# A quarter of the additions of states into y in a selective-scan kernel go from VectorE to ScalarE and GpSimd

## The reference

```python
u, gate = split(xn @ W_in.T)                       # D = 1024 channels each
u = silu(causal_conv4(u) + conv_b)
dt, B, C = (rmsnorm(p) for p in split(u @ Wx.T))    # 32, N = 16, N = 16
delta = softplus(dt @ Wdt.T + dt_bias)
state = exp(delta * A) * state + delta * u * B      # for each of D x N states, along 512 tokens
y = sum over n of C[n] * state[n]  +  u * D_param
s = (y * silu(gate)) @ W_out.T
g = silu((silu(xn @ w_gate.T) * (xn @ w_up.T)) @ w_down.T)
x = x + s * g
```

## Time and profile before

| | us |
|---|---|
| median of 3 runs | 1310.66 (1310.46 to 1311.51) |
| the profiled execution | 1310.51 |
| its span, first to last instruction | 1308.6 |
| VectorE busy | 1160.3 (89%) |
| TensorE busy | 1109.4 (85%) |
| GpSimd busy | 950.5 (73%) |
| ScalarE busy | 665.7 (51%) |

### The profile page before, as it was taken

One profiled execution on the slowest core, in us unless ns is written; L12 is line 12 of the kernel. 1 busy time (PEld: TensorE's weight loads), 2 busy tenths in 40 slices (PEclk: granted clock), 3 DMA queues, 4 the chain that ended last, 5 costly groups with the idle time before them and its releaser, 6 DMA issues.

```text
span 1308.6 us, 16506 instructions
## 1 busy us (share of the span) xinstructions
PE 1109.4 (85%) x5072; PEld 777.8 (59%) x5072; DVE 1160.3 (89%) x1436; ACT 665.7 (51%) x1000; POOL 950.5 (73%) x440
## 2 busy tenths in 40 slices
PE   5859985789959987988987997998995998986977
PEld 4647764655647765564656765665564776544544
DVE  5359999998979999999798999999797999999893
ACT  4557543654476643465375843465447664443330
POOL 3488985777678996577579897576767899755731
PEclk9879996699969998999997999899996999996979
DMA  4112231212302231322222232232221222221411
GB/s 131 66 49 88 88 117 38 66 56 73 105 28 95 89 129 49 129 81 91 79 76 79 76 121 81 93 109 73 73 105 28 94 90 97 90 96 57 129 48 65
DMA packets 42789, 108.78 MB, mean 83 GB/s; under 512 B 4843, under 2 KB 5099, under 8 KB 42700
## 3 DMA queue, kind: packets, MB, share of 16 engines
q1 hardware_dynamic: 42700, 107.69, 24.8%
HBM read 103.35 MB, written 4.33 MB: 82 GB/s over the span
## 4 chain that ended last, share of the span: by engine, by line
PE 31%; DVE 24%; POOL 22%; issue 17%; ACT 3%; DMA 1%; DVEq 1%; POOLq 0%
POOL sb_dBu L578 13%; DVE sb_h L816 11%; PE pj L861 8%; PE pj L1069 7%; DVE sb_yT L742 6%; PE hT L1109 6%; PE pj L1093 3%; POOL sb_v L550 3%; POOL sb_delta L544 3%; DVE sb_un L661 3%; POOL sb_w_lo L533 2%; PE pj L1123 2%; PE pj L1036 2%; PE pj L866 2%; PE pj L878 1%
## 5 line engine op out<-in xcount | busy, mean ns | idle before, releaser
L578 POOL TENSOR_TENSOR sb_dBu<-sb_v,sb_bb 128x1024 f32<-128x1024 f32 x256 | 607.4, 2388 | 166.2 <-DVE sb_h L816 161.5
L816 DVE TENSOR_TENSOR_SCAN sb_h<-dA,sb_dBu 128x512 f32<-128x512 f32 x512 | 595.7, 1204 | 46.6 <-POOL sb_dBu L578 28.9
L439 ACT ACTIVATE dA<-sb_delta,sb_apar 128x512 f32<-128x512 f32 x512 | 352.4, 691 | 543.4 <-DVE sb_h L816 538.1
L1109 PE MATMUL hT<-sb_ident,sb_h 128*128 128x128 f32 x2048 | 310.0, 294 | 145.2 <-DVE sb_yT L742 128.0
L1109 PEld LDWEIGHTS hT<-sb_ident,sb_h 128*128 128x128 f32 x2048 | 251.8, 150 | 247.4 <-DVE sb_yT L742 137.9
L742 DVE SCALAR_TENSOR_TENSOR sb_yT<-hT,sb_cs,sb_yT 128x512 f32<-128x512 f32 x476 | 330.1, 734 | 35.7 <-PE hT L1109 35.0
L533 POOL TENSOR_TENSOR sb_w_lo<-sb_ring,sb_w_hi 128x1024 fp32r<-128x1024 f32 x76 | 181.6, 2390 | 79.9 <-ACT sb_w_hi L331 79.5
L861 PE MATMUL pj<-sb_x_hi,sb_w_lo 128*128 128x512 f32 x608 | 188.6, 434 | 26.6 <-DVE sb_un L661 16.3
L861 PE MATMUL pj<-sb_x_lo,sb_w_hi 128*128 128x512 f32 x608 | 172.3, 407 | 0.0
L861 PE MATMUL pj<-sb_x_hi,sb_w_hi 128*128 128x512 f32 x608 | 165.9, 395 | 0.0
L861 PEld LDWEIGHTS pj<-sb_x_hi,sb_w_lo 128*128 128x128 f32 x608 | 108.5, 198 | 74.6 <-issue 22.6
(11 more groups left out here) (100 smaller groups left out, 819.0 us busy)
## 6 DMA issues: line engine op xcount, KB each, us to landing
sb_ring<-w_ring SPq DMA_DIRECT2D x116, 512.0 KB, 3.3
sb_bb<-b_rows SPq DMA_DIRECT2D x128, 256.0 KB, 3.2
sb_xio<-x SPq DMA_DIRECT2D x8, 1024.0 KB, 6.4
out<-sb_xio SPq DMA_DIRECT2D x3, 1024.0 KB, 5.6
out<-sb_xio SPq DMA_DIRECT2D x4, 256.0 KB, 2.0
sb_wx<-w_x SPq DMA_DIRECT2D x1, 256.0 KB
sb_wdt<-w_dt SPq DMA_DIRECT2D x1, 132.0 KB
b_rows<-sb_dtB SPq DMA_DIRECT2D x4, 32.0 KB, 1.6
```

Source lines behind the costliest of these rows:

```text
L439: nc.scalar.activation(dA[g % 2][:, :], delta[:, j, :], ACT.Exp, scale=apar[:, j, n:n + 1]).then_inc(dA_done, 1)
L578: nc.gpsimd.tensor_tensor(dBu[:, dbu_buffer(s), :, :], v[:, j:j + 2, :], bb[:, i % B_RING, :].unsqueeze(1).to_broadcast([P, 2, T]), ALU.mu ...
L816: nc.vector.tensor_tensor_scan(h[:, i % 2, 2 * part + e, :], dA[g % 2][:, :], dBu[:, dbu_buffer(s), e, :], 0.0, ALU.mult, ALU.add).then_in ...
L1109: done = nc.tensor.transpose(hT[c % H_BANKS][:, j * P:(j + 1) * P], h[:, i % 2, j, c * P:(c + 1) * P], ident[:, :])
```

## The change

Block c = 3 of each unit is handed over (`handed_over` returns (3,) for every unit). VectorE adds blocks 0, 1 and 2 as before. For block 3 ScalarE multiplies the transposed block by C (Copy with a scale by partition, from a copy cs_act of C of its own) in its slot 2i + 3, after `side` and ahead of `round_entry`: for n = 0 straight into yT, else into one of two buffers `part`. GpSimd adds the buffer to yT in its slot 2i + 5, after dBu and w_lo and ahead of the gate products. Of unit 31 of the last batch nothing is handed over. TensorE waits for ScalarE's semaphore `ev_done` where the bank was freed by a product, and for GpSimd's `yp_done` as well before it transposes y back. In batches 1 to 3 the products of unit 31 fall into slot 1, and the sums of units 30 and 31 into slots 1 and 3. To make room in SBUF, the conv buffer cth is laid over the first two tiles of v.

```diff
+def handed_over(u):
+    return (3,)
+OFF = [(u, c) for u in range(UNITS) for c in handed_over(u)]
+OFF_ADDS = [(u, c) for u, c in OFF if u % N > 0]
+ON = [(u, c) for u in range(UNITS) for c in range(TC) if (u, c) not in OFF]
...
-        cth = sb("cth", [P, 2, T])
+        part = sb("part", [P, 2, H])
+        cs_act = sb("cs_act", [P, TC, N])
...
+        cth = v[:, 0:2]
...
+                def take_state(c_b, i, c, no_first):
+                    hf, n = i // N, i % N
+                    act.wait_ge(hT_ps, c_b * UNITS * TC + i * TC + c + 1)
+                    if n == 0:
+                        if not no_first:
+                            act.wait_ge(yb_ps, (c_b - 1) * KD + (hf + 1) * JH)
+                        dst = yT[:, c, hf * JH * P:(hf + 1) * JH * P]
+                    else:
+                        q = OFF_ADDS.index((i, c))
+                        if not (no_first and q < 2):
+                            act.wait_ge(yp_done, c_b * len(OFF_ADDS) + q - 1)
+                        dst = part[:, q % 2, :]
+                    nc.scalar.activation(dst, hT[c % H_BANKS][:, :], ACT.Copy, scale=cs_act[:, c, n:n + 1]).then_inc(ev_done, 1)
...
                 for s in range(SLOTS):
                     decay(s)
                     side(s)
+                    for i, c in OFF:
+                        if s == 2 * i + 3:
+                            take_state(b, i, c, first)
+                        elif s == 2 * i + 3 - SLOTS and not first:
+                            take_state(b - 1, i, c, False)
+                    if s == 2 and not first:
+                        act.wait_ge(nrm_done, (b + 1) * 2)
+                        act.wait_ge(ev_done, b * len(OFF))
+                        nc.scalar.copy(cs_act[:, :, :], nrm[:, :, G + N:FN]).then_inc(csa_done, 1)
+                        act.wait_ge(csa_done, b + 1)
                     if s in HI_AT and not (last and HI_AT[s][1] >= U0):
                         round_entry(b, *HI_AT[s])
...
+            def add_part(c_b, i, c):
+                q, hf = OFF_ADDS.index((i, c)), i // N
+                pool.wait_ge(ev_done, c_b * len(OFF) + done_by(OFF, i, c))
+                before = [p for p in range(q) if OFF_ADDS[p][1] == c and OFF_ADDS[p][0] // N == hf]
+                if before:
+                    pool.wait_ge(yp_done, c_b * len(OFF_ADDS) + before[-1] + 1)
+                y = yT[:, c, hf * JH * P:(hf + 1) * JH * P]
+                nc.gpsimd.tensor_tensor(y, y, part[:, q % 2, :], ALU.add).then_inc(yp_done, 1)
...
+                    for m, c in OFF_ADDS:
+                        if s == 2 * m + 5:
+                            add_part(b, m, c)
+                        elif s == 2 * m + 5 - SLOTS and not first:
+                            add_part(b - 1, m, c)
...
-                        if i > 0:
+                        if i > 0 and (i - 1, c) in ON:
                             add_state(b, i - 1, c)
-                        elif not first:
+                        elif i == 0 and not first and (UNITS - 1, c) in ON:
                             add_state(b - 1, UNITS - 1, c)
...
                         if j == JH:
-                            pe.wait_ge(y_done, b * UNITS * TC)
+                            pe.wait_ge(y_done, b * len(ON))
+                            pe.wait_ge(yp_done, b * len(OFF_ADDS))
                             pe.wait_ge(za_done, b * KD + JH)
```

More of the change, by code:

```diff
@@ L49, with done_by @@
 ORDINAL = {k: o for o, k, s in SPLITS}
+def handed_over(u):
[3 more added lines that the diff above has]
+ON = [(u, c) for u in range(UNITS) for c in range(TC) if (u, c) not in OFF]
+def done_by(acts, u, c):
+    return len([a for a in acts if a <= (u, c)])
 def dbu_buffer(s):
@@ L614, in _ @@
             sequences(pool, sequence)
+            for m, c in OFF_ADDS:
+                if SLOTS <= 2 * m + 5 and m < UNITS - 1:
+                    add_part(NB - 1, m, c)
             for j in range(JH, KD):
@@ L829, in _ @@
                 dve.wait_ge(hT_ps, b * UNITS * TC + i * TC + c + 1)
-                dve.wait_ge(y_done, b * UNITS * TC + (i - 1) * TC + c + 1)
+                if (i - 1, c) in ON:
+                    dve.wait_ge(y_done, b * len(ON) + done_by(ON, i - 1, c))
+                else:
+                    dve.wait_ge(yp_done, (b + 1) * len(OFF_ADDS) - len(handed_over(i)) - len(handed_over(i - 1)) + done_by([(i - 1, d) for d in handed_over(i - 1)], i - 1, c))
                 y = yT[:, c, JH * P:D]
@@ L1105, in sequence @@
                     for c in (2 * part, 2 * part + 1):
-                        if not (first and i == 0 and c < 2):
-                            pe.wait_ge(y_done, b * UNITS * TC + i * TC + c - 1)
+                        before = (i, c - H_BANKS) if c >= H_BANKS else (i - 1, c + TC - H_BANKS)
+                        if not first or before[0] >= 0:
+                            if before in ON or (UNITS - 1, before[1]) in ON and before[0] < 0:
+                                pe.wait_ge(y_done, b * len(ON) + (done_by(ON, *before) if before[0] >= 0 else done_by(ON, UNITS - 1, before[1]) - len(ON)))
+                            else:
+                                pe.wait_ge(ev_done, b * len(OFF) + (done_by(OFF, *before) if before[0] >= 0 else done_by(OFF, UNITS - 1, before[1]) - len(OFF)))
                         for j in range(JH):
```

15 lines of the change are left out of this document (11 added, 4 removed).

## The result

The changed kernel takes 1339.0 us (median of 4 runs, 1337.2 to 1339.9), the kernel before 1311.1 beside it (4 runs, 1310.5 to 1312.1). The ratio is 1.021 (95% interval 1.019 to 1.023): slower by 28 us, where 1318.0 was forecast with 1337 as the upper end. The profiled execution has a span of 1338.1 us, against 1308.6.

What follows compares the result with a forecast made beforehand. The bound was taken to change by slot: GpSimd in 14 to 20, VectorE in 21 to 27 and 39 to 46, TensorE in 28 to 38 and 47 to 60. +15.0 + 18.0 - 25.4 = +7.6 us gave 1318, range 1299 to 1337.

Steps and rivals of the forecast that it cites:

- Slots 15 to 21: All four batches: sums of slots 15, 17 and 19 delay dBu of slot 21, 3 x 1.25 us each: +15.0 us.
- Slots 0 to 14 with the end of the batch before: Batch start: sums and a later w_hi(8) delay dBu(15), 5.5 us in three batches and 1.5 in batch 0: +18.0 us.
- I take +5.5: Batches 1 to 3: slot 15 late by 5.7 us, VectorE's lead taking up some, so +5.5 each; batch 0 +1.5.
- The count of GpSimd's queue behind w_lo(8): From w_lo(8) to dBu(15): 12 x 2.36 us, four gate products and the sums of 9, 11 and 13, 37.1 us.
- This is what the order product, then rounding costs: Batches 1 to 3: w_hi(8), queued behind unit 2's product on ScalarE, comes at 726.2 where it came at 722.6.
- Slots 21 to 60: Where VectorE holds the others up, 39 spared additions of 0.65 us count: -25.4 us; in 47 to 60 savings become waiting.
- priced as a rival: 12 scalings of x within the loops all meet GpSimd, 2.587 instead of 1.494 us: +13.1 us, 1331; chance 0.05.
- ScalarE holds the decays: Product waits for TensorE ahead of the next decay; scan 0.5 us later in 39 units: 19.5 us, 1337; chance 0.08.
- the faster rival: Slots 0 to 14: GpSimd's lead and idle time cover all sums, the 18.0 us fall away: 1300; chance 0.20.
- TensorE gives way: TensorE's 4.31 us slots have hidden waits, so 14 more savings count, 9.1 us: 1309; chance 0.12.
- the signs named for it: Signs of a right forecast: waits on hT grow in slots 28 to 38 and 47 to 60, which keep their lengths.
- TensorE would wait for GpSimd's sum at y's transposes: Slot 1: a sign of a right forecast, TensorE waiting for GpSimd's sum at the transposes of y; no size given.

Runs made afterwards that it cites:

- the sum alone: The kernel before, all additions on VectorE and no product, plus one unread 128x512 sum on GpSimd in the changed kernel's slots, 30 a batch: 1341.3 us.

## Why the prediction was wrong in size

The sign and the place of the costs were right; the sum was +7.6 where the span grew by 29.5. Of the 21.9 us between them 11.0 lie in slots 0 to 14 with the end of the batch before, 9.6 in savings that did not come, 1.8 before and behind the loops, and −0.6 in slots 15 to 20. Term by term:

- **Slots 15 to 21: +15.0 forecast, +14.4 measured.** Three sums of 1.25 in each batch, with GpSimd's queue full, and the sum alone costs the same 14.4. VectorE's wait for dBu in a unit was to grow from 1.0 to more than 2.5 us; it is 2.77 (the first scan of slot 17 of batch 2, after), for a dBu that ends at 793.60:

```profile
791.23 2.37 POOL L637 TENSOR_TENSOR sb_dBu<-sb_v,sb_bb 128x1024 f32<-128x1024 f32 x1
...
793.72 1.22 DVE L883 TENSOR_TENSOR_SCAN sb_h<-dA,sb_dBu 128x512 f32<-128x512 f32 x1 [2.77 <-POOL sb_dBu L637]
```

- **Slots 0 to 14 with the end of the batch before: +18.0 forecast, +29.0 measured (25.4 + 3.6).** This is the failed step, the term "I take +5.5" and "+1.5" for batch 0. The count of GpSimd's queue behind w_lo(8) held: 37.1 us forecast; measured 38.4 in batch 2 (744.63 to 783.00), 1.44 of which is a wait for a rounding, w_hi(14), that the step had left out for batches 1 to 3 (the kernel before has it with 0.79). The granted clock, which the prediction did not count, has a part in it. TensorE waits 2.77 us for the late w_lo(12), and from 769.60 to 773.10 its granted clock is 0.51, the level of 1.2 GHz. Four of its products take 1.91 us there where four such take 1.07 at 774.88, and the next four 1.87; the transposes, ScalarE's product and the rounding stand behind them. In slots 8 to 13 the clock is 1.00 before and with the rounding first, 0.94 in after:

```profile
768.62 1.25 PE L931 MATMUL pj<-sb_x_hi,sb_w_lo 128*128 128x512 f32 x4 [2.77 <-POOL sb_w_lo L583]
769.66 1.91 PE L931 MATMUL pj<-sb_x_lo,sb_w_hi 128*128 128x512 f32 x4
```

  w_lo(8) itself (744.63) came 4.3 us later instead of 3.6 against the batch's first scan, and not by waiting for its own rounding: GpSimd had lost the time to two earlier ones, w_hi(4) (2.32 us, at 728.20 above) and w_hi(6) (1.06 us). The measured delay of dBu(15) is 7.6 us in batch 2 and 6.2 to 7.6 in batches 1 to 3, where the softplus part comes on top with 1.0 to 1.4 instead of 0.8. In batch 0 it is 5.1, not 1.5.
- **The sentence that fell** is "A product behind which ScalarE's decay is queued costs nothing as long as the transposes are there early in the slot". Its condition held in the slots that I had looked at (17 to 19). In slots 3 to 13 TensorE has hardly any idle time, as the first part of the prediction says itself, so the transposes end late in the slot, as at 726.38 above. And what stands between product and decay is not nothing but the rounding, 1.04 us. "This is what the order product, then rounding costs" was seen for one entry and priced once, at 0.65 + 1.03; it acts from slot 3 on, at one rounding after the other, and by way of GpSimd: VectorE's waits for dBu in slots 3 to 14 of all batches grew from 1.0 to 18.6 us, and are 5.7 with the rounding first. Those for dA grew from 2.0 to 17.5, and 13.4 of them stay with the rounding first, so they are not what that order wins. The runs give it 15 us: 25.4 against 9.6 with the rounding first and 10.2 with no product at all. With that order, the kernel takes 1321.0, and the forecast was 1318.0. That this is so near is in part luck: of the forecast's +18.0 for the front 13.3 are measured then, and of its −25.4 only −18.1.
- **Slots 21 to 60: −25.4 forecast, −15.8 measured.** Each saving is worth what was said: −2.6 in slots 39 to 46 of every batch, four times 0.65. What is missing is missing in slots 21 to 27, 11.0 us (−10.4 forecast, +0.6 measured); the stages behind gave 1.4 more than forecast. VectorE is busy nearly throughout there, so its own rows account for it, over all batches: its additions into y fell by 10.5 us as forecast, the scalings of x grew by 5.3, three additions over 128x4 by 2.1 (last section), waits for dBu and dA by 2.8, the scans by 0.7. The scalings had been priced as a rival (+13.1 if all 12 meet GpSimd at full length), with a chance of 0.05, and left out of the sum. The price took the median for each of the 12; they took 21.3 us together before, so it should have been about +10. Yet the row that gave its bounds, 532 to 2587 ns with a median of 1494, already showed that scalings meet GpSimd before the change, and the change adds 1.28 us to GpSimd's queue right there; it had to be a term, not a mishap.
- **The rivals.** "ScalarE holds the decays" was put at 0.08 in VectorE's own slots. It happened elsewhere: of the 40 us by which the waits for dA grew, 15.5 lie in slots 3 to 14, 17 in slots 47 to 63, where TensorE sets the pace and slots 47 to 60 got no longer, and 4.3 in slots 21 to 46, the ones that the rival was about. GpSimd's lead does take up something: the sum alone costs nothing in slots 8 to 13 (25.87 against 25.69), but 5.1 us then come in slot 14 and 4.7 had come in slots 0 to 2, so the faster rival (1300) fell. "TensorE gives way" fell too, as 28 to 38 of batches 1 and 2 kept their lengths. Of the signs named for it, the waits on hT grew in slots 28 to 38 (2.0 to 6.7 us) but not in 47 to 60 (28.7 to 27.6); those for dA grew there instead (1.3 to 13.0).
- **The count of sums.** 127 products less the eight with n = 0 are 119 sums, not 120; it changes nothing.
- **TensorE would wait for GpSimd's sum at y's transposes.** Not seen. In batch 2 of after they run right behind the transposes of h (725.35, above), with no idle time:

```profile
726.22 0.60 PE L993 MATMUL pj<-sb_ident,sb_yT 128*128 128x128 f32 x4
```

The sum of unit 31 began at 722.28 and took 1.27 us, so it was there. TensorE was late for other reasons by then, among them a wait of 0.84 us for w_lo at 720.13.
